# Expert outputs scattered to token order by GpSimd during the tiles, and read back by plain SyncE transfers

## The reference, cut to what matters

```python
# layer 2: mixture of 8 experts, two of them per token
probs = softmax(xf @ Wr); weights, indices = top_k(probs, 2)
for e in range(8):
    h = gelu(xf @ W1[e]) @ W2[e]
    coeff = sum(where(indices == e, weights, 0))
    out = out + coeff[:, None] * h
h = h + out
# layer 3 begins: state-space block on layernorm(h)
xz = x @ W_in ; conv ; silu ; delta = softplus(...) ; scan over time ; y @ W_out
```

## Time and profile before

| | us |
|---|---|
| median of 3 runs (lowest, highest) | 4184.95 (4178.12, 4190.71) |
| the profiled execution | 4172.62 |
| its span, first to last instruction | 4170.9 |
| sending stage, first send to the tiles' first load | 2092.5 to 2217.0 |
| tiles, to the last copy's end | 2217.0 to 2565.9 |
| state-space block: first instruction, first `logarithm` | 2568.9, 2698.2 |

### The profile page before, as it was taken

One profiled execution on the slowest core, in us unless ns is written; L12 is line 12 of the kernel. 1 busy time (PEld: TensorE's weight loads), 2 busy tenths in 40 slices (PEclk: granted clock), 3 DMA queues, 4 the chain that ended last, 5 costly groups with the idle time before them and its releaser, 6 DMA issues. The chain is left out here.

```text
span 4170.9 us, 70241 instructions
## 1 busy us (share of the span) xinstructions
PE 3284.4 (79%) x23447; PEld 2210.8 (53%) x23448; DVE 2086.2 (50%) x4029; ACT 1232.1 (30%) x2459; POOL 1221.4 (29%) x934
## 2 busy tenths in 40 slices
PE   7589981649997699999606996478888887579999
PEld 3357761326775367777505995234334333256777
DVE  0444437323445245555542333478888888731443
ACT  2222110011121122222213442265555565413222
POOL 0102110102120124334171002656556555510221
PEclk9698875778888899999658998689888888769998
DMA  1000000570000200000241112222212221100000
GB/s 46 12 1 0 0 2 11 88 97 1 0 0 11 88 1 0 0 0 0 70 137 50 45 50 60 74 58 54 52 46 58 52 52 52 36 10 0 9 11 10
DMA packets 250482, 140.02 MB, mean 34 GB/s; under 512 B 175329, under 2 KB 226467, under 8 KB 250384
## 3 DMA queue, kind: packets, MB, share of 16 engines
q1 hardware_dynamic: 230480, 122.61, 12.0%
q0 software_dynamic: 18432, 12.40, 1.3%
q10 hardware_dynamic: 1472, 3.85, 0.3%
HBM read 103.41 MB, written 35.21 MB: 33 GB/s over the span
## 5 line engine op out<-in xcount | busy, mean ns | idle before, releaser
L2414 DVE TENSOR_TENSOR_SCAN ssm_state<-ssm_dA,ssm_dBx 128x372 f32<-128x372 f32 x512 | 434.3, 910 | 103.3 <-ACT ssm_dA L2203 82.6
L2109 POOL TENSOR_TENSOR ssm_dBx<-ssm_du,ssm_bc_wide 128x1488 f32<-128x1488 f32 x128 | 426.9, 3340 | 196.5 <-DVE ssm_state L2414 195.1
L2288 PE MATMUL ssm_y<-ssm_hC,top_ident 128*128 128x512 f32 (+1 forms) x768 | 405.9, 671 | 93.8 <-DVE ssm_hC L2419 86.6
L2203 ACT ACTIVATE ssm_dA<-ssm_delta,ssm_decay 128x368 f32<-128x368 f32 x512 | 276.7, 565 | 190.9 <-DVE ssm_state L2414 179.2
L2288 PEld LDWEIGHTS ssm_y<-ssm_hC,top_ident 128*128 128x128 f32 x768 | 157.6, 216 | 307.9 <-issue 165.2
L2419 DVE TENSOR_TENSOR ssm_hC<-ssm_state,ssm_c_wide 128x1488 f32<-128x1488 f32 x128 | 218.1, 1704 | 5.1
L643 ACT ACTIVATE dattn_probs<-dattn_scoresT 93x372 f32<-93x372 f32 x256 | 108.1, 472 | 350.9 <-PE dattn_scoresT L556 350.9
L570 PE MATMUL dattn_outputs<-dattn_v,dattn_probs 93*93 (+1 forms) x2048 | 185.4, 233 | 0.0
L570 PEld LDWEIGHTS dattn_outputs<-dattn_v,dattn_probs 93*93 93x93 f32 x2048 | 181.8, 163 | 3.4
L489 POOL TENSOR_TENSOR rattn_q<-rattn_q_all,rattn_only 128x372 f32<-128x372 f32 x64 | 51.7, 807 | 439.6 <-PE rattn_scoresT L556 247.2
L1409 POOL TENSOR_TENSOR dattn_square<-dattn_square,top_minus_half 93x16 f32<-93x16 f32 x32 | 92.7, 2896 | 271.9 <-DVEq L1485 271.9
(11 more groups left out here) (546 smaller groups left out, 7209.1 us busy)
## 6 DMA issues: line engine op xcount, KB each, us to landing
ssm_bc_wide<-bc_rows SPq DMA_DIRECT2D x128, 372.0 KB, 4.3
route_stage<-in_L_ffn_W SPq DMA_DIRECT2D x32, 512.0 KB, 4.2
qkv_rows<-rattn_rows SPq DMA_DIRECT2D x32, 288.0 KB, 3.1
rattn_heads<-qkv_rows SPq DMA_DIRECT2D x96, 96.0 KB, 3.5
moe_sent<-top_blank SPq DMA_DIRECT2D x1, 7936.0 KB, 23.6
tiles_x_in<-moe_sent SPq DMA_DIRECT2D x31, 256.0 KB, 2.8
moe_back<-tiles_y SPq DMA_DIRECT2D x31, 256.0 KB, 2.1
tok_frames<-in_frames ACTq DMA_DIRECT2D x8, 376.0 KB, 8.4
```

What stands on the lines that cost most here:

```text
L2109: pool.tensor_tensor(dBx[:, k % 2, :, :], du[:, :, :], bc_wide[:, q % BUFS, 0, k % 2, :].unsqueeze(1).broadcast_to([P, CC, GT]), ALU.mult) ...
L2203: act.activation(by_utterance(dA[:, ring(k, c), 0:GT])[:, :, 1:], by_utterance(delta[:, c, :])[:, :, 1:], ACT.Exp, scale=decay[:, c, k:k + ...
L2288: mm = pe.matmul(ps_y[:, at], ident[:, :], hC[:, k % 2, :, :].rearrange("p c t -> p (c t)")[:, at], start=(k == 0), stop=(k == N - 1), ski ...
L2414: dve.tensor_tensor_scan(state[:, k % 2, c, :], dA[:, ring(k, c), 0:GT], dBx[:, k % 2, c, :], 0.0, ALU.mult, ALU.add).then_inc(scanned, 1)
```

## The change

Each sent row becomes 260 values wide (`SENT`): 256 of the token and one that holds its home, 1 + 2·token + k, as a number (the other three are zero). DVE therefore writes each utterance's rows twice, side by side, and copies two columns of homes into them. In the tiles DVE works out the home of each loaded row; an empty row (home 0) gets a spare row of its own at the tensor's end. POOL, not SP, stores `y`: two indirect DMAs of 128 rows per tile, each row to its home. So `moe_back` is in token order with both expert rows of a token side by side, and the state-space block reads it with SP: per utterance one transfer of 80 token rows and one of 13, each row 2 KB, five utterances in flight. The first five stand before the weight loads, the others behind them. POOL has no gathers there any more. DVE's loop over the tiles is now written out.

```diff
 def dispatch
+        sent_rows = s.sb("sent_rows", [P, SENDING, 2, SENT])
+        n = Norm(s, shared["stat"], xn=sent_rows[:, :, 0, 0:D])
+        home = s.sb("home", [P, B, 2])
+                pool.memset(sent_rows[:, :, :, D:], 0.0).then_inc(const_ready, 1)
+                pool.iota(home[:, :, :], [[2 * T, B], [1, 2]], base=1, channel_multiplier=2, ...)
-                    pool.wait_ge(rows_ready, b + 1)
+                    pool.wait_ge(rows_ready, 2 * b + 2)
-                                                n.xn[0:T, b % SENDING, :], None, ...
+                                                sent_rows[0:T, b % SENDING, k, :], None, ...
-                    dve.tensor_scalar(n.xn[rows, b % SENDING, :], hidden[rows, b, :], ...
+                    dve.tensor_copy(sent_rows[rows, b % SENDING, :, D], home[rows, b, :]).then_inc(rows_ready, 1)
+                    dve.tensor_scalar(sent_rows[rows, b % SENDING, :, 0:D], hidden[rows, b, :].unsqueeze(1).broadcast_to([T, 2, D]), ...
 def expert_tiles
                 def load(t, j):
                         sync.wait_ge(x_turned, t - 1)
+                        sync.wait_ge(home_ready, t - 1)
-                def store(t, j):
-                    sync.wait_ge(y_copied, t + 2)
-                    sync.dma_start(rows_of(back, t), y[:, j, :, :]).then_inc(y_stored[j], 16)
+                for j in range(2):
+                    sync.wait_ge(y_stored[j], 16 * HALVES * ((TILES + 1 - j) // 2))
             def _(pool):
-                for j in range(2):
-                    pool.wait_ge(y_stored[j], 16 * ((TILES + 1 - j) // 2))
+                pool.iota(spare[:, :, :], ...).then_inc(spare_ready, 1)
+                for t in range(TILES):
+                    pool.wait_ge(home_ready, t + 1)
+                    pool.wait_ge(y_copied, t + 2)
+                    for h in range(HALVES):
+                        pool.indirect_dma_start(back, bass.IndirectOffsetOnAxis(home[:, t % 4, h:h + 1], 0), y[:, t % 2, h, :], ...
                 def take(t, j):
                     dve.wait_ge(x_high, t + 1)
+                    if t >= 4:
+                        dve.wait_ge(y_stored[j], 16 * HALVES * (t // 2 - 1))
+                    dve.scalar_tensor_tensor(stray[:, :], x_in[:, j, :, D], 0.0, spare[:, t, :], ALU.is_equal, ALU.mult)...
+                    dve.wait_ge(stray_ready, t + 1)
+                    dve.tensor_tensor(home[:, t % 4, :], x_in[:, j, :, D], stray[:, :], ALU.add).then_inc(home_ready, 1)
 def state_space
-    FETCHED = 8
+    FETCHED = 5
             def _(sync):
+                def fetch(b):
+                    if b >= FETCHED:
+                        sync.wait_ge(summed, 2 * (b - FETCHED) + 2)
+                    for lo, hi in ((0, 80), (80, T)):
+                        sync.dma_start(got[lo:hi, b % FETCHED, :], back[1 + 2 * (b * T + lo):1 + 2 * (b * T + hi), :]...
+                for b in range(FETCHED):
+                    fetch(b)
                 (eleven weight loads)
+                for b in range(FETCHED, B):
+                    fetch(b)
             def _(pool):
-                for m in range(3 * GU):
-                    fetch(m)
                 first_root(0, 0, GU)
-                for m in range(3 * GU, 2 * B):
-                    fetch(m)
                 first_root(1, GU, B)
```

More of the change, by code:

```diff
@@ L1543 @@
 ROWS = HALVES * P
+SENT = D + 4
 TILES = (2 * B * T + EXPERTS * (ROWS - 1)) // ROWS
@@ L1744, in _ @@
                         dve.wait_ge(rows_sent[b % SENDING], 32 * (b // SENDING))
-                    dve.tensor_scalar(n.xn[rows, b % SENDING, :], hidden[rows, b, :], n.mean[rows, b:b + 1], n.rstd[rows, b:b + 1],
-                                      ALU.subtract, ALU.mult).then_inc(rows_ready, 1)
+                    dve.tensor_copy(sent_rows[rows, b % SENDING, :, D], home[rows, b, :]).then_inc(rows_ready, 1)
+                    dve.tensor_scalar(sent_rows[rows, b % SENDING, :, 0:D], hidden[rows, b, :].unsqueeze(1).broadcast_to([T, 2, D]),
+                                      n.mean[rows, b:b + 1], n.rstd[rows, b:b + 1], ALU.subtract, ALU.mult).then_inc(rows_ready, 1)
                     if G + 2 + b < JOBS:
@@ L1790, in load @@
                         sync.wait_ge(x_turned, t - 1)
+                        sync.wait_ge(home_ready, t - 1)
                     sync.dma_start(x_in[:, j, :, :], rows_of(sent, t)).then_inc(x_loaded[j], 16)
-                def store(t, j):
-                    sync.wait_ge(y_copied, t + 2)
-                    sync.dma_start(rows_of(back, t), y[:, j, :, :]).then_inc(y_stored[j], 16)
                 load(0, 0)
                 load(1, 1)
-                for t in range(TILES):
-                    if t < TILES - 2:
-                        load(t + 2, t % 2)
-                    if t:
-                        store(t - 1, (t - 1) % 2)
-                store(TILES - 1, (TILES - 1) % 2)
+                for t in range(TILES - 2):
+                    load(t + 2, t % 2)
+                for j in range(2):
+                    sync.wait_ge(y_stored[j], 16 * HALVES * ((TILES + 1 - j) // 2))
             @block.gpsimd
             def _(pool):
-                for j in range(2):
-                    pool.wait_ge(y_stored[j], 16 * ((TILES + 1 - j) // 2))
+                pool.iota(spare[:, :, :], [[ROWS, TILES], [P, HALVES]], base=1 + 2 * B * T, channel_multiplier=1,
+                          allow_small_or_imprecise_dtypes=True).then_inc(spare_ready, 1)
+                for t in range(TILES):
+                    pool.wait_ge(home_ready, t + 1)
+                    pool.wait_ge(y_copied, t + 2)
+                    for h in range(HALVES):
+                        pool.indirect_dma_start(back, bass.IndirectOffsetOnAxis(home[:, t % 4, h:h + 1], 0), y[:, t % 2, h, :], None,
+                                                bounds_check=2 * B * T + TILES * ROWS).then_inc(y_stored[t % 2], 16)
             @block.scalar
@@ L1906, in tile @@
                         keep(t - 1, 1 - j)
+                dve.wait_ge(spare_ready, 1)
                 take(0, 0)
-                over_tiles(dve, tile)
+                for t in range(TILES):
+                    tile(t, t % 2, t == TILES - 1)
                 keep(TILES - 1, (TILES - 1) % 2)
@@ L2314, in add @@
                         m = 2 * b + k
-                        dve.wait_ge(got_loaded[m % FETCHED], 16 * (m // FETCHED + 1))
+                        dve.wait_ge(got_loaded[b % FETCHED], 32 * (b // FETCHED + 1))
                         if k:
                             dve.wait_ge(summed, m)
-                        dve.scalar_tensor_tensor(hidden[0:T, b, :], got[0:T, m % FETCHED, :], share[0:T, k, b:b + 1], hidden[0:T, b, :],
+                        dve.scalar_tensor_tensor(hidden[0:T, b, :], got[0:T, b % FETCHED, k * D:(k + 1) * D], share[0:T, k, b:b + 1], hidden[0:T, b, :],
                                                  ALU.mult, ALU.add).then_inc(summed, 1)
```

43 lines of the change are left out of this document (23 added, 20 removed).

## The result

| | us |
|---|---|
| before, median of 12 runs (lowest, highest) | 4184.66 (4178.12, 4190.71) |
| changed kernel, median of 12 runs (lowest, highest) | 4173.04 (4166.01, 4185.62) |
| ratio | 0.9978, 95% interval 0.9968 to 0.9988 |
| profiled execution, before and after | 4172.62 and 4170.24 |

The gain is 0.22%, about 9 us (5 to 13), where 27 were forecast. The time lies inside the stated range, but the change is a third of the forecast, and less than the 0.3% that "faster" stood for.

What follows compares the result with a forecast made beforehand. GpSimd was taken to bound the sends, TensorE the tiles, and gathers, through VectorE's order, the state-space block's start. 0.4 + 4.8 + 1.0 + 4.9 - 38.4 = -27.3 us from the median 4184.95 gave 4158, range 4140 to 4179.

Steps and rivals of the forecast that it cites:

- Before the sends: Ahead of the first send, GpSimd's new memset and iota were to cost +0.4 us (0 to 4.6).
- The sends: Sending stage: VectorE's longer row operation was to delay 12 sends by 0.4 us each, +4.8 us (0 to 12.8).
- a rule: Skill page: one-input, plain-rate VectorE operations don't hold up sends; sum then near -32, but stretched rows were held against it.
- the rival on the other side: Sending stage: GpSimd pays for the wider row, each send could double, +56.5 us in all, 4241; chance 0.08.
- The tiles: First two tiles +1.0 us (0 to 2) for VectorE's new operations and wider loads; middle tiles nothing, scatters hidden.
- The end of the tiles: Last copy to the next block: two scatters in place of a store, 8.0 us, so +4.9 (3.8 to 9).
- the engines' meeting: End of the tiles: some 0.6 us between the last landing and the next block's start.
- The start of the state-space block: Block's start to logarithm: weights at 16.5, norm 16.7 later, then 57.6 unchanged; 90.9 us, 38.4 earlier.
- the change touches three stages: Opening step: only sending, tiles and the state-space block's start were taken as affected by the change.
- The fetch did not stay last: State-space block: rival that plain transfers deliver no faster than gathers, gain only 8.4 us, time 4188; chance 0.08.
- the row operation's own price did hide: Sending stage: rival that the row operation hides wholly, without the 4.8 us, time 4153; chance 0.12.
- the upper ends of the costs: Rival over all stages: every cost at its upper end and gain 36.2, sum -11.2 us, so 4174; chance 0.12.

Runs made afterwards that it cites:

- the two kernels that change that stretch: Changed kernel, each fetch from utterance 9 waiting for the add just before: 4185.67 us; changed kernel with gamma moved, blank padded, first five fetches on ACT's queue: 4140.06 us.
- the first pair: First profiled executions of the kernel before and the changed kernel, without further edits: 4172.62 and 4170.24 us.
- the slowed fetch: Changed kernel with each fetch from utterance 9 on waiting for the add just before it, not the fifth before: 4185.67 us, logarithm at 119.6 us.
- the padded one: Changed kernel with blank padded to 272 values, 64 bytes more than before instead of 16: 4165.30 us, ratio to before 0.9928.
- the seam without either side effect: Changed kernel with gamma loads ahead of the clearing and blank at 272 values, 4135.56 us, against the kernel before with gamma moved, 4168.79: 0.74%, 31 us.
- The kernels with 64 bytes: Changed kernels with blank moved by a multiple of 64 bytes; padding alone gave 4165.30 us, with gamma loads ahead of the clearing too 4135.56 us.

## Why the prediction was wrong

**The seam's sum was right, in part by luck.** Over all profiles (six of kernels with the old seam, eight with the new one) the stretches are:

| stretch | old seam, mean (range) | new seam, mean (range) | difference | forecast |
|---|---|---|---|---|
| to the first send | 65.3 | 66.0 | +0.7 | +0.4 |
| sending | 126.3 (123.2 to 128.8) | 128.6 (123.6 to 131.1) | +2.3 | +4.8 |
| tiles | 348.4 (347.7 to 349.0) | 348.7 (348.1 to 349.4) | +0.4 | +1.0 |
| end of the tiles | 3.0 | 9.4 | +6.4 | +4.9 |
| to the logarithm | 129.1 (128.4 to 130.1) | 91.9 (90.9 to 92.9) | -37.2 | -38.4 |

(The last row leaves out the two kernels that change that stretch.) Together -27.4, where -27.3 had been worked out. That it agrees to a tenth is luck: the parts are off by 0.3 to 2.5 us, and the errors cancel. Step by step:

- *Before the sends.* Right: the iota takes 0.48 us, and the first send is no later than that and the memset make it.

```profile
2058.73 0.48 POOL L1624 IOTA route_home<- 128x64 f32 x1
```

- *The sends.* The +4.7 of the first pair looked like a confirmation of +4.8 and is not one: either kernel spreads over 5 to 8 us from one execution to the next, and the means differ by 2.3. The row operation takes 0.54 us, not 0.68: its 256 further columns cost 0.13 us, half of what the forecast took from `low`, which is another kind of operation. So it does not run at the plain rate for which the forecast weighed a rule, and the stretched rows of before are no evidence against that rule. Sends without VectorE beside them take 1.31 as ever, so the wider row costs GpSimd nothing, and the rival on the other side falls.

```profile
L1636 POOL DMA_INDIRECT moe_sent<-route_sent_rows,top_slot x64: 1306/1310/3278, 2123.9 to 2246.1; - x64
...
DMA to landing us min/median/max: 4.0/4.9/7.7
```

```profile
L1752 DVE TENSOR_SCALAR route_sent_rows<-top_hidden,route_mean,route_rstd x32: 532/536/992, 2122.1 to 2238.1; 93x512 f32<-93x512 f32 x32
```

What holds up sends is `low`, not the row operation. In the kernel before, a send with a row operation alone beside it took 1.41 us, and one with a `low` beside it 2.12:

```profile
2195.44 0.41 DVE L1745 TENSOR_SCALAR route_xn<-top_hidden,route_mean,route_rstd 93x256 f32<-93x256 f32 x1 [3.25 <-DMA moe_sent<-route_xn,top_slot]
...
2195.62 1.41 POOL L1630 DMA_INDIRECT moe_sent<-route_xn,top_slot  x1 [0.30 <-issue]
```

```profile
2146.17 1.20 DVE L1682 TENSOR_TENSOR moe_w<-route_stage,moe_w 128x1024 bf16<-128x1024 f32 x1
2146.44 2.12 POOL L1630 DMA_INDIRECT moe_sent<-route_xn,top_slot  x1 [0.30 <-DVE route_xn L1745]
```

Summed over the sends behind the first, what exceeds 1.31 us beside row operations alone is 0.1 to 0.4 us in any of the fourteen profiles. Beside `low` it is 10.1 to 15.6 us with the old seam and 12.5 to 20.3 with the new one (means 13.2 and 17.6), and the stage takes just this and 113 us, or 111 with the new seam, in every profile. So the spread is that of the meetings with `low`. The 2.3 are 4.5 more of these, less 2.6 by which the first send became shorter (3.28 for 5.88), and not a price of the longer row operation per meeting, as the forecast had it.

- *The tiles.* Right, hidden; the cost at the first two tiles is below what the runs can tell. A scatter of 128 rows is faster than a send of 93, 0.97 us, and lands in 2.4:

```profile
L1820 POOL DMA_INDIRECT moe_back<-tiles_y,tiles_home x62: 967/974/1312, 2280.8 to 2603.4; - x62
...
DMA to landing us min/median/max: 2.4/2.4/2.8
```

- *The end of the tiles.* The size was off by 1.4 us. That it was no more is luck: the scatters are shorter and land sooner than the sends from which they were sized, and the engines' meeting is longer. The timeline of the last tile on VectorE and GpSimd:

```profile
2600.58 0.69 DVE L1913 COPY tiles_y<-tiles_product 128x512 f32<-128x512 f32 x1 [4.55 <-PE tiles_product L1537]
...
2602.11 0.97 POOL L1820 DMA_INDIRECT moe_back<-tiles_y,tiles_home  x1 [2.99 <-DVE tiles_y L1913]
2603.39 0.97 POOL L1820 DMA_INDIRECT moe_back<-tiles_y,tiles_home  x1 [0.30 <-issue]
2610.78 0.20 POOL L2088 MEMSET ssm_ones<- 128x128 f32 x1 [6.42 <-POOLq L69]
```

The scatters are over at 2604.36 and landed some 1.4 us later, but the next block begins at 2610.70. The sending stage of before ended in the same manner: last send over at 2210.2 + 1.31 = 2211.5, first load of the tiles at 2216.96, 5.4 us later. A stage that ends with GpSimd's own transfers had its price in the trace of before, and the forecast took the meeting of the engines (0.6) from a stage that ended with a plain store instead. Counted from the last landing, the next stage began 0.9 us behind that store, 2.1 behind the sends, and 4.9 behind the scatters now; why the scatters take longer than the sends is open.

- *The start of the state-space block.* The size is right in each of its three parts. The reason of the weights' delay was not the issues on SyncE's queue, from which its 2.4 us were taken, so that this size came out is luck.

**The step that failed is the first one**: "the change touches three stages". The sum put the other stages at nothing and so left out two lines of the diff that act there, both about `blank`. The wider row of `moe_sent` is also what is cleared in layer 2, some 740 us before its first use, and there ACT waits for loads queued behind the clearing: **+3.5 us**, in every profile of the changed kernel with that order and a single-row clearing. And `blank` itself is allocated for the whole program, so that four more values of it move every later tile of SBUF by 16 bytes. In layer 1's attention, where TensorE waits for the transfers to `rattn_heads`, that costs **+14 us** (169.9 us from the first to the last in four profiles without the shift, 184.0 in six with 16 or 32 bytes), and 1.0024 of the time (+10 us, 5 to 16) where it is the only edit.

-27.4 + 3.5 + 14.1 = -9.8 us. The medians of the two kernels differ by 11.6, and the ratio's interval is -5 to -13 us. No closer agreement can be asked: three stretches outside the account vary with the granted clock, that behind layer 1's transfers by 9 us over the profiles, the rest of layer 2's attention by 22, the last layer by 8. The other two kernels fit within their noise: -23.9 by the account for the padded one, where -30 (-21 to -39) was measured, and -27.4 for the seam without either side effect, where it was 31. That the changed kernel's time lies inside the stated range is luck as well, for neither of the two costs is in the sum.

None of the rivals was the one that came true. The fetch did not stay last (20.7 us of slack, and the slowed fetch shows what it would have cost); the sends did not double; the row operation's own price did hide, as one of them had it, but its time did not come, and more meetings with `low` took 2.3 us in place of the 4.8; the upper ends of the costs, which would have given a like time, did not occur.

## What to carry to other kernels

List all allocations and all uses of every tensor whose shape a diff changes, not only the stages that it means: its initialisation is work too, with a queue behind it, and a tile that outlives the stage moves all that is allocated after it. Keep the sizes of such long-lived tiles at the multiples they had (64 bytes here), or compare the landings of unrelated transfers before and after. And a stretch of one pair of profiles that agrees with a forecast confirms it only where repeats of the same kernel agree among themselves: the sends' +4.7 did not, the logarithm's -38.4 did.

## What the runs showed of the hardware beyond that

- **SBUF addresses and DMA.** `rattn_heads` receives sixteen pieces of 16 values (64 bytes) per partition and transfer. With the tile moved by 16 or 32 bytes the transfer lands in 4.9 us, without or with 64 bytes in 3.4 to 3.5. A tile with long rows didn't show it: `tiles_x_in`, with 1,024 or 1,040 bytes per row, lands in 2.6 to 2.9 us in all profiles. Shifts by the length of a piece are the ones that cost nothing; why is not shown.
- **The kernels with 64 bytes** are also below the old placement in layer 1's attention: 532 to 537 us in four profiles, 537 to 540 in four of the old. The landings are alike, and so is the time from the first transfer to the last. The difference lies behind these: that part takes 349.4 to 350.4 us in nine profiles, at a granted clock of 0.84, and 341.5 to 344.9 in five, at 0.86. The changed kernel itself is in both groups (350.4 and 341.5 in its two profiles), so it isn't the placement; what sets the clock there is open.
- **The last layer** takes 528.2 or 528.3 us in all six profiles of kernels with the old seam, and 523 to 532 with the new one. The windows of its last part, before and then after, differ in the granted clock, 0.78 and 0.94 of full speed, so in how the stretch is shared between the two levels of 1.2 and 2.4 GHz (columns as in the earlier trace rows):

```profile
4123.00:4171.00 48.00, 40.67 (x339) 31.13 (x338) 13.27 (x37) 8.66 (x24) 3.30 (x8) 0.78 0.03 10
```

```profile
4125.00:4168.00 43.00, 36.12 (x355) 27.77 (x351) 13.62 (x38) 9.23 (x26) 4.01 (x8) 0.94 0.04 11
```

What in the changed kernel moves the clock so far behind the change wasn't tried. It changes the last layer by -5 to +3 us and is not in the account above, which leaves as much room.

- **The spread between executions** of one kernel, 13 to 36 us in the sets of six runs and more, sits mostly in the rest of layer 2's attention: 634 to 656 us over the fourteen profiles, with the granted clock falling from 0.97 in the shortest to 0.93 in the longest. A single execution of each kernel, 4172.62 against 4170.24, would have said that the change does nothing.
